# Weighted sums of values in a cross-attention kernel: how a PSUM bank's columns are opened

## The reference, cut to what matters

```
weights = softmax(where(mask == 0, NEG, q @ k.T / sqrt(32)))   # per head, 77 keys
out = weights @ v                                              # per head, 32 columns
x = x + tanh(g_xattn) * (out @ Wo.T)
x = x + tanh(g_ffn) * bitlinear_ffn(layernorm(x))              # w_gate, w_up, w_down
```

## Time and profile before

| | us |
|---|---|
| median of 3 runs | 1356.69 |
| lowest and highest run | 1356.05 and 1358.62 |
| the profiled execution | 1358.6 |
| its span in the trace | 1356.8 |
| PE busy | 1260.9 (93%) |
| DVE busy | 1144.6 (84%) |
| ACT busy | 878.1 (65%) |
| POOL busy | 735.1 (54%) |

### The profile page before, as it was taken

One profiled execution on the slowest core, in us unless ns is written; L12 is line 12 of the kernel. 1 busy time (PEld: TensorE's weight loads), 2 busy tenths in 40 slices (PEclk: granted clock), 3 DMA queues, 4 the chain that ended last, 5 costly groups with the idle time before them and its releaser, 6 DMA issues.

```text
span 1356.8 us, 26014 instructions
## 1 busy us (share of the span) xinstructions
PE 1260.9 (93%) x7424; PEld 630.1 (46%) x7998; DVE 1144.6 (84%) x2631; ACT 878.1 (65%) x1350; POOL 735.1 (54%) x1187
## 2 busy tenths in 40 slices
PE   4776799999999999999999999999999999999996
PEld 2223444545454454545454454545445454544542
DVE  6877597898979798897979799797979989797884
ACT  5886747557584756758575665758475675847663
POOL 2113645546574664657465564756456465746662
PEclk8978899999999999999999999999999999999998
DMA  9785346574653647364564646455464736445333
GB/s 341 223 247 112 75 104 140 110 163 107 148 135 105 138 102 186 97 156 110 131 148 94 161 108 153 107 140 132 105 152 108 180 94 150 121 113 116 90 79 73
DMA packets 386793, 181.64 MB, mean 134 GB/s; under 512 B 324323, under 2 KB 357987, under 8 KB 385123
## 3 DMA queue, kind: packets, MB, share of 16 engines
q1 hardware_dynamic: 386736, 181.04, 55.1%
HBM read 61.32 MB, written 35.46 MB: 71 GB/s over the span
## 4 chain that ended last, share of the span: by engine, by line
PE 58%; DVE 29%; issue 5%; DMA 3%; ACT 3%; POOL 1%; SPq 1%; POOLq 0%; ACTq 0%; DVEq 0%
PE bank L1244 21%; PE bank L1256 15%; PE bank L1185 5%; DVE region L1046 5%; PE bank L1105 4%; DVE nmax L985 4%; PE bank L1106 3%; PE bank L1107 3%; DVE xh L975 3%; DVE xbig L1013 2%; DVE hmx L1052 2%; DVE st L1017 2%; DVE xn L970 2%; PE bank L1207 1%; PE bank L1209 1%
## 5 line engine op out<-in xcount | busy, mean ns | idle before, releaser
L628 POOL TENSOR_TENSOR region<-region,up 128x512 f32<-128x512 f32 x256 | 344.7, 1350 | 140.5 <-DVE region L1046 80.0
L1244 PE MATMUL bank<-tern_gate,region 128*128 128x512 fp8e4 x1024 | 264.8, 381 | 8.4 <-DMA region<-zb 7.3
L1244 PE MATMUL bank<-tern_up,region 128*128 128x512 fp8e4 x1024 | 263.8, 380 | 0.2 <-ACT up L781 0.2
L1256 PE MATMUL bank<-tern_down,region 128*128 128x512 fp8e4 x1024 | 234.0, 382 | 10.1 <-DMA region<-hb 9.4
L773 ACT ACTIVATE region<-bank,fs 128x512 f32<-128x512 f32 x256 | 177.4, 697 | 83.5 <-PE bank L1244 83.1
L1046 DVE SCALAR_TENSOR_TENSOR region<-region,bank 128x512 f32<-128x512 f32 x256 | 173.4, 682 | 59.9 <-ACT region L773 54.7
L1052 DVE TENSOR_REDUCE hmx<-region 128x1 f32<-128x512 f32 x256 | 170.7, 678 | 56.3 <-POOL region L628 56.2
L619 POOL TENSOR_TENSOR work<-work 124x512 f16<-124x512 f32 x160 | 191.7, 1220 | 28.7 <-ACT work L742 28.5
L582 POOL TENSOR_TENSOR rs<-mv,lnc 128x1 f32<-128x1 f32 (+1 forms) x80 | 26.7, 334 | 290.8 <-DVE mv L1020 274.0
L781 ACT ACTIVATE up<-bank 128x512 f32<-128x512 f32 x256 | 152.7, 612 | 19.6 <-PE bank L1244 18.8
L786 ACT ACTIVATE hb<-region 128x2048 bf16<-128x2048 f32 x64 | 122.7, 1918 | 56.0 <-DVE region L1068 56.0
(11 more groups left out here) (144 smaller groups left out, 2393.7 us busy)
## 6 DMA issues: line engine op xcount, KB each, us to landing
q_stack<-q_rows SPq DMA_DIRECT2D x96, 256.0 KB, 5.1
xbig<-in_x SPq DMA_DIRECT2D x16, 1024.0 KB, 5.4
q_rows<-q SPq DMA_DIRECT2D x64, 256.0 KB, 2.0
out_y<-o SPq DMA_DIRECT2D x64, 256.0 KB, 3.3
q_stack<-mT SPq DMA_DIRECT2D x32, 256.0 KB, 3.7
region<-in_wgT SPq DMA_DIRECT2D x4, 1024.0 KB, 8.3
region<-in_wuT SPq DMA_DIRECT2D x4, 1024.0 KB, 7.2
region<-in_wdT SPq DMA_DIRECT2D x4, 1024.0 KB, 5.9
```

The lines of the kernel that those rows point to most:

```text
L628: nc.gpsimd.tensor_tensor(ht, ht, up[:, n % 2, :], ALU.mult).then_inc(hmul_ready, 1)
L1244: ins = T.matmul(pb[2 * (n % 2) + w][:, :], xqT[:, k, tok], tern[w][:, k * FF + n * GT:k * FF + (n + 1) * GT], start=(k == 0), stop=(k == ...
L1256: ins = T.matmul(pb[2][:, :], hT[:, t % 2, k, :], tern[2][:, k * GT:(k + 1) * GT], start=(k == 0), stop=(k == FK - 1))
```

## The change

Chunks are worked in the order 0, 2, 4, 1, 3. Chunks 0, 2 and 4 share no head, and each writes its two heads' columns with its first product; only that of chunk 0 carries `start=True`. Chunks 1 and 3 hold three heads, of which the outer two have been written by then; the first product of such a chunk is issued in two parts, one with the 33 columns of the middle head, which nothing has written yet, and one with the 66 columns of the outer two. The product with `v_none` is gone, and with it the tile and its memset on POOL; the number that other engines wait for on `cast_ready` goes down by one.

```diff
+CHUNKS = [c for c in range(0, CH, 2)] + [c for c in range(1, CH, 2)]
...
-        v_none = sb("v_none", [CR, (HH - len(SPANS[0])) * HW], f16)
...
-                sp.wait_ge(cast_ready, 5 + 3)
+                sp.wait_ge(cast_ready, 4 + 3)
...
-            nc.gpsimd.memset(v_none[:, :], 0.0).then_inc(cast_ready, 1)
...
-                for cc in range(CH):
+                for cc in CHUNKS:
                     heads = len(SPANS[cc])
                     o = SPANS[cc][0][0] * HW
                     dst = bank[:, o:o + heads * HW].rearrange("p (h n) -> p h n", n=HW)
                     both = v[:, hf, V_AT[cc]:V_AT[cc + 1]].rearrange("p (h n) -> p h n", n=VW)
                     hi, lo = (p[0:CR, CH * hf + cc, tok] for p in (p_hi, p_lo))
-                    if cc == 0:
-                        T.matmul(bank[:, heads * HW:HH * HW], hi, v_none[:, :], start=True, stop=False)
-                    T.matmul(dst, hi, both[:, :, 0:HW], start=False, stop=False)
+                    if cc % 2 == 0:
+                        T.matmul(dst, hi, both[:, :, 0:HW], start=(cc == 0), stop=False)
+                    else:
+                        T.matmul(dst[:, 1, :], hi, both[:, 1, 0:HW], start=False, stop=False)
+                        T.matmul(dst[:, 0::2, :], hi, both[:, 0::2, 0:HW], start=False, stop=False)
                     T.matmul(dst[:, :, 0:DH], hi, both[:, :, HW:VW], start=False, stop=False)
-                    ins = T.matmul(dst, lo, both[:, :, 0:HW], start=False, stop=(cc == CH - 1))
+                    ins = T.matmul(dst, lo, both[:, :, 0:HW], start=False, stop=(cc == CHUNKS[-1]))
                 ins.then_inc(pv_mm, 1)
```

More of the change, by code:

```diff
@@ L638, in turn @@
                     pieces[part][name](at[part], i, j)
-            pool.wait_ge(cast_ready, 5 + 3)
+            pool.wait_ge(cast_ready, 4 + 3)
             turn(POOL_FIRST, *FRONT)
@@ L662, in head_rows @@
                 act.wait_ge(consts_in, 16 * 5)
-                act.wait_ge(cast_ready, 5 + 3)
+                act.wait_ge(cast_ready, 4 + 3)
                 nc.scalar.activation(k_heads[96:P, :, 0:NK].rearrange("p (h c) n -> p h c n", h=HC),
```

## The result

The changed kernel takes 1379.7 us (median of 4 runs, 1377.42 to 1380.64), the kernel before 1356.37 beside it (4 runs, 1352.64 to 1358.62). The ratio is 1.0173, its 95% interval 1.0153 to 1.0193: **slower by 23 us**, where 4.9 us less had been forecast. The profiled execution took 1380.1 us, with a span of 1378.3.

A forecast was written before the change was run, and what follows sets the result against it. PE was taken to bound most of a group and DVE the rest. Savings of 4.3 us (13 middle groups), 0.4 (last turn) and 0.2 (front) sum to 4.9 us, from 1356.69 to 1351.8; range 1347.5 to 1356.7.

The forecast's parts named there:

- The cost of one call: On PE at full clock, a call of `weighted` becomes 0.067 us shorter, between 0.057 and 0.087.
- third rival: Pairs of weight load and matmul have a fixed price, so calls get longer: +4.0 us, 1360.7; chance 0.04.
- `down00` moves by 0.27 + 0.06 = 0.33 us: In each middle group PE's `down00` starts 0.33 us earlier, limited by DVE's line 1046; 13 groups save 4.3 us.
- second rival: Other small limits on the engines take most of the gain: 1.8 us left, 1354.9; chance 0.20.
- The sign that I named: On PE, some 0.14 us more than usual between the call's last product and `down00`'s first, waiting for line 1046.
- The eighth call's gain falls into PE's spare time: nothing: Behind `down00`, where DVE bounds the group, the eighth call is off the chain and its shortening saves nothing.
- fourth rival: Behind 333 us DVE meets POOL anew, as at line 1009: some 0.5 us per group, +1.6 us in all; chance 0.08.
- shift together: From 333 us DVE and POOL both run on DVE's own releases, which spoke against a new meeting.
- The removed tile: On POOL, the memset of `v_none` (0.26 us) was followed by 2.98 us of idle time, so it costs nothing.
- The gap ahead of line 1074: DVE's idle time before line 1074, behind `down00`, should shrink from 0.41 to about 0.15 us.
- The other turns: Outside the middle groups: nothing in the second turn, 0.4 us saved in the last, 0.2 in the front.
- Range and chances: 1347.5 to 1356.7 us; 0.68 on faster by over 0.2%, 0.22 on within 0.2%, 0.10 on slower.

The follow-up runs named there:

- f1: The changed kernel with 160 bytes of padding behind `v`, and POOL's last product for `up23` waiting for DVE's `hq`: 1354.66 us, ratio 0.9984.
- e6: The kernel before, its addresses too, with the new form of the call only in the eighth call of each group: 1369.18 us, ratio 1.0103.
- e2: The kernel before, every instruction kept, with `v_none` allocated last so that tiles lie as in the changed kernel: 1386.07 us, ratio 1.0181.
- g1: The changed kernel with only the wait of POOL's last `up23` product for DVE's `hq`, no padding: 1368.54 us, ratio 1.0099.
- g4: The changed kernel with only the 160 bytes of padding behind `v`, no added wait: 1366.27 us, ratio 1.0073.
- f3: f1 without the product of high values with low values of `v` in each group's first seven calls: 1351.81 us, ratio 0.9969.

## Why the prediction was wrong, by its steps

- **The cost of one call**: right. 0.57 for 0.65 us, and the 33-column product at 0.02 to 0.03. The third rival, a fixed price for a pair, is refuted.
- **"`down00` moves by 0.27 + 0.06 = 0.33 us"**: too much. I looked for the second condition of `down00` among semaphores of DVE, and took line 1046 for it. Its input comes by a transposing DMA, and that had 0.12 us to spare. Sum for 13 groups: 13 x 0.17 = 2.2 us, not 4.3. And only 12 groups can gain, 2.0 us: rows 7, which I read as the second turn, are the first middle group's, where the chain comes through the landing already. f1's measured gain is 2.2 us (1.0 to 3.4), nearest in size to the second rival's 1.8, by another cause. The sign that I named, some 0.14 us more than usual ahead of `down00`, came (0.12 to 0.25 in f1), but from the landing and not from line 1046.
- **"The eighth call's gain falls into PE's spare time: nothing"**: the step that failed in kind. The gain was nothing, the shift was not: some 0.07 us of PE time tipped a meeting and cost 1.07 us in each of 12 groups, 12.1 us in all (e6 shows it alone; in the change the moved tiles would have tipped it too, as in e2). The fourth rival named this mechanism with a chance of 0.08, but at line 1009 and at 0.5 us. Against it I wrote that both engines "shift together" behind 333 us; but ACT's `up23` and with it POOL's product follow PE there, not DVE. A look at what ends and starts within 0.1 us of each other on the chain would have shown it: `up23` ends at 350.63, `hq` starts at 350.71. I also narrowed the rule to two-input instructions, where the same sentence of the Trainium skill covers 2-port modes, and `hq` takes 1.29 us for 2048 columns, less than half of 4 x 0.68, line 1046's time for 512.
- **The removed tile**: costed as a memset that costs nothing. It had a second effect that no term covered, the addresses of all tiles behind it: 15.6 us, the larger part (g1's median is 2.3 us over g4's). No view of the profile shows an address; the diff does show an allocation gone.
- **The gap ahead of line 1074**, forecast at 0.15 us: 0.53 in the change, 0.38 in f1. Not even in f1 is it what I said, since `down00` moved by half.
- **The other turns** (+0.6 us gain): not separable in the change. In g1 the front alone loses 4.65 us against f1, a size that varies from trace to trace as said above. The landing of `hb` that rows 7 showed, 5.29 us, is not what differs: it is 4.99 us in g1 and 4.93 in f1. On the chain ahead of it `aT` lands in 4.61 us against 3.70, and the first `zb` in 4.93 against 4.19.
- **Range and chances**: 1347.5 to 1356.7 missed by 23 us, with 0.10 on slower. Both losses lay outside the terms, so no width given to the terms would have held the result.

## What to carry to other kernels

A diff that adds or removes an SBUF tile moves every tile behind it: compare the addresses of all tiles that DMAs read or write, modulo 256 (the built program lists them), before the change is judged, and pad where a remainder has changed. When a few hundredths of a us move on one engine, look for VectorE and GpSimd instructions on long SBUF operands whose starts lie within 0.1 us of each other, and settle the winner by a wait. And for each point where a gain should arrive, go through all its conditions, the landing of its DMA too, before the gain is counted.

## What was not expected of the hardware

- Two of the four transposing DMAs within SBUF land 0.5 to 0.6 us later (3.7 to 4.3 for hb, 2.7 to 3.3 for xh) when their tiles start 64, 96 or 128 bytes past a multiple of 256 rather than at one; for ah it is 0.1 us, and zb doesn't follow its own tiles.
- An engine that is 0.94 us less busy per group (f3 against f1) leaves the period as it is, and a product of POOL of 1.27 us that comes some 0.1 us earlier against `hq` makes it 1.07 us longer.
- DVE's line 1063, a product of one column, takes 1.12 us beside a POOL product, its neighbour 1064 takes 0.15.
- The long `hq` does not appear as a wait: in the chain it is the "issue" row that grows, from 1.16 us to 2.14, because an instruction that is held up is recorded as longer, not as later.
